# Attentions 3 and 4 of a four-layer perceiver: where a head's sums are folded and divided, and in which order TensorE issues a head's steps

## The reference, cut to what matters

```
q = (layernorm(x) @ Wq.T + bq) per head;  k = (ctx @ Wk.T + bk);  v = (ctx @ Wv.T + bv)
scores = q @ k.T / sqrt(16)                 # 256 x 4096 for each of 16 heads
attn   = softmax(scores, axis=-1)
x      = x + (attn @ v) @ Wo.T + bo
```

## Time and profile before

| what | value |
|---|---|
| median of 3 runs | 1447.46 us |
| profiled execution | 1446.92 us, its span 1445.7 us |
| TensorE / VectorE / ScalarE / GpSimd busy | 87% / 71% / 59% / 33% of the span |
| attention 3, from the first maximum to the last division | 927.28 to 1118.69 us |
| attention 4, the same | 1210.55 to 1401.97 us |
| VectorE busy from 953 to 1098 us | 139.1 of 145 us |
| granted TensorE clock from 953 to 1098 us | 1.00 |

### The profile page before, as it was taken

The page is one execution under the profiler, slowest core; times in us unless marked ns, Lnnn a source line. Parts: engine busy times, 40 slices in busy tenths (PEclk is TensorE's granted clock), DMA queues, the critical chain, the costliest instruction groups (busy, mean ns, idle before and its releaser), DMA issues. The chain is left out here.

```text
span 1445.7 us, 29634 instructions
## 1 busy us (share of the span) xinstructions
PE 1258.0 (87%) x10855; PEld 633.9 (44%) x10930; DVE 1020.2 (71%) x2341; ACT 851.7 (59%) x1339; POOL 482.2 (33%) x678
## 2 busy tenths in 40 slices
PE   6899786999998786799999888599998895999987
PEld 5566451333333355133333554244444582444445
DVE  4868578999998435788886153499994336999932
ACT  4632127999998330388888451178886212788852
POOL 1421314899889603244444240111110001111100
PEclk9999895999999989599999999789999997999999
DMA  8598781211122020111223336212144201122300
GB/s 319 157 318 291 217 296 42 56 38 38 44 58 97 3 72 22 46 41 54 56 51 124 124 71 218 65 47 65 56 126 142 73 0 43 56 64 67 114 2 8
DMA packets 115175, 136.62 MB, mean 95 GB/s; under 512 B 13579, under 2 KB 96179, under 8 KB 112956
## 3 DMA queue, kind: packets, MB, share of 16 engines
q1 hardware_dynamic: 107142, 126.55, 28.4%
q10 hardware_dynamic: 7888, 8.16, 1.7%
HBM read 99.73 MB, written 34.90 MB: 93 GB/s over the span
## 5 line engine op out<-in xcount | busy, mean ns | idle before, releaser
L1263 ACT ACTIVATE prob_a<-ps 128x1024 f32<-128x1024 f32 x480 | 468.6, 1020 | 97.4 <-PE ps L1086 57.4
L1068 PE MATMUL ps<-kop,qop 52*128 52x512 f16 x1024 | 302.2, 418 | 64.4 <-DMA qop<-qparts 21.3
L1287 DVE TENSOR_REDUCE best_a<-ps 128x1 f32<-128x512 f32 (+1 forms) x488 | 317.8, 709 | 25.0 <-PE ps L1068 22.9
L1086 PE MATMUL ps<-qop,kop 52*128 52x256 f16 x2048 | 217.8, 280 | 6.2 <-ACT prob_a L1263 2.7
L1115 PE MATMUL ps<-prob_a,vop_a 128*32 128x256 f32 x3072 | 212.8, 399 | 4.8 <-issue 4.7
L1283 DVE CUSTOM_DVE_ANT_0 dump_a<-ps,neg_q 128x512 bf16<-128x512 f32 (+1 forms) x244 | 165.8, 715 | 42.7 <-PE ps L1068 41.5
L1068 PEld LDWEIGHTS ps<-kop,qop 52*128 52x128 f16 x1024 | 73.1, 95 | 247.1 <-DVE best_a L1287 96.6
L1401 POOL TENSOR_TENSOR used_a<-prob_a,gT 128x1024 f32<-128x1024 f32 x64 | 154.1, 2409 | 24.0 <-DVE used_a L1300 19.4
L1379 POOL TENSOR_SCALAR mrest_a<-nmax_a 128x2 f32<-128x2 f32 x64 | 27.9, 435 | 332.9 <-DVE nmax_a L1292 332.9
L1086 PEld LDWEIGHTS ps<-qop,kop 52*128 52x128 f16 x2048 | 92.1, 96 | 105.6 <-issue 53.4
L1115 PEld LDWEIGHTS ps<-prob_a,vop_a 128*32 128x32 f32 x3072 | 86.0, 112 | 90.6 <-issue 58.1
(11 more groups left out here) (382 smaller groups left out, 1755.3 us busy)
## 6 DMA issues: line engine op xcount, KB each, us to landing
kop<-kparts SPq DMA_DIRECT2D x384, 64.0 KB, 2.3
vals<-vst SPq DMA_DIRECT2D x16, 1024.0 KB, 5.8
kparts<-kp SPq DMA_DIRECT2D x64, 256.0 KB, 4.2
vraw<-vals SPq DMA_DIRECT2D x64, 256.0 KB, 3.0
e_w<-in_e_w SPq DMA_DIRECT2D x4, 2048.0 KB, 11.5
z_w<-in_z_w SPq DMA_DIRECT2D x24, 256.0 KB, 7.0
gT<-in_ctxT SPq DMA_DIRECT2D x8, 512.0 KB, 12.5
raw<-in_mask SPq DMA_DIRECT2D x16, 256.0 KB, 3.9
```

Of the source, the lines that this page charges most:

```text
L1068: return pe.matmul(out, qop[rows, h, t * P:(t + 1) * P], kop[rows, h % UNROLL, first:first + CHUNK], start=True, stop=True)
L1086: ins = pe.matmul(st_bank(n)[:, j * NT:(j + 1) * NT], kop[rows, h % UNROLL, at:at + P], qop[rows, h, :], start=(j % 2 == 0), stop=(not add ...
L1263: act.activation(prob[:, n % NP, :], st_bank(n), ACT.Exp, scale=1.0 / SCORE_UNIT).then_inc(S("exp_done"), 1)
L1287: dve.tensor_reduce(out, bank, AX.X, ALU.max).then_inc(sem, 1)
```

## The change

Six edits, all for attentions 3 and 4 (`not by_query`):

- **F into bank 7.** For heads 0 to 14 (`aside`) the folded sums go into the first 64 columns of bank 7, over the sums that have been read, and not into the ring. F takes no place among the chunks any more.
- **ScalarE takes them out** (`read_fold`): one copy of 128 x 64 from PSUM to `folded_sums`, right behind `place_max`. V3 has to wait for it too, as it opens new sums in the same bank.
- **GpSimd divides** (`divide`): a power of -1 of the 128 x 2 denominators and a multiply of 128 x 32, behind the head's `split` and `fill`. The last head is divided by VectorE as before.
- **`AHEAD` is 26** and not 24: 13 pairs at the start, and the last chunk of head h+1 is now the 6th C of head h.
- **`TURN_AT` is 4** and not 5: `place_max` stands behind the fifth exponential of a head and not the sixth.
- **A new `PLAIN_ORDER`**: F and T stand together behind C10, V's are spread differently.

```diff
-PLAIN_ORDER = "CCKKCCV CKCKCCV KCKCF CCTCKKCV CCV".replace(" ", "")
+PLAIN_ORDER = "CCKKCV CKCCKCV CKCCFTKCCKCV CKCCV".replace(" ", "")
...
-    AHEAD = 32 if weighted else 24
+    AHEAD = 32 if weighted else 24 if by_query else 26
...
-    SUM_AT, TURN_AT = (1, 1) if weighted else (3, 4) if by_query else (3, 5)
+    SUM_AT, TURN_AT = (1, 1) if weighted else (3, 4) if by_query else (3, 4)
...
+    aside = lambda h: not by_query and h < H - 1
...
+    fold_out = c.ps[:, 7, 0:QT * 32]
...
                     if h > 0:
                         pe.wait_ge(S("sums_read"), h)
+                    if h > 0 and aside(h - 1):
+                        pe.wait_ge(S("fold_read"), h)
...
         def fold(h):
 
-            bank = ring_bank()
+            bank = fold_out if aside(h) else ring_bank()
             pe.wait_ge(S("sums_read"), h + 1)
...
-            ins.then_inc(S("s_psum"), 1)
+            ins.then_inc(S("folded" if aside(h) else "s_psum"), 1)
...
+        def read_fold(h):
+
+            act.wait_ge(S("folded"), h + 1)
+            if h > 1:
+                act.wait_ge(S("divided"), h - 1)
+            act.activation(folded_sums[:, h % 2, :, :], fold_out.rearrange("p (t e) -> p t e", t=QT), ACT.Copy)\
+               .then_inc(S("fold_read"), 1)
...
                 if g == TURN_AT and h + 1 < H:
                     place_max(h + 1)
+                if g == TURN_AT and h > 0 and aside(h - 1):
+                    read_fold(h - 1)
...
-                elif step == "F" and h > 0:
+                elif step == "F" and h > 0 and not aside(h - 1):
                     normalise(h - 1)
...
+        def divide(h):
+
+            pool.wait_ge(S("fold_read"), h + 1)
+            pool.tensor_tensor(rden[:, h % 2, :], folded_sums[:, h % 2, :, HD], minus_one[:, :], ALU.pow).then_inc(S("inverted"), 1)
+            pool.wait_ge(S("inverted"), h + 1)
+            pool.tensor_tensor(c.att[:, :, HD * h:HD * (h + 1)], folded_sums[:, h % 2, :, 0:HD],
+                               rden[:, h % 2, :].unsqueeze(2).to_broadcast((P, QT, HD)), ALU.mult).then_inc(S("divided"), 1)
...
             if not SHARED and 0 < h < H - 1:
                 fill(h + 1)
+            if h > 0 and aside(h - 1):
+                divide(h - 1)
```

More of the change, by code:

```diff
@@ L1002, in attend @@
     rden = sb("rden", [P, 2, QT], F32)
+    folded_sums = None if by_query else sb("folded_sums", [P, 2, QT, 32], F32)
+    minus_one = None if by_query else sb("minus_one", [P, QT], F32)
     dump = sb("dump", [P, 1, CHUNK] if weighted else [P, 2, 2 * CHUNK], BF16) if by_query else None
@@ L1194, in _ @@
         stage.reads = slots.n
+        stage.divided = 0 if by_query else H - 1
     @stage.scalar
@@ L1249, in _ @@
                     at += 1
-                if step == "F" and h > 0:
+                if step == "F" and h > 0 and not aside(h - 1):
                     slots.next()
@@ L1311, in normalise @@
                 dve.wait_ge(S("den_added"), h + 1)
+            if not by_query:
+                dve.wait_ge(S("divided"), H - 1)
             dve.reciprocal(rden[:, h % 2, :], den[:, h % 2, :] if weighted else folded[:, :, HD]).then_inc(S("den_inverted"), 1)
-            dve.wait_ge(S("den_inverted"), h + 1)
+            dve.wait_ge(S("den_inverted"), h + 1 if by_query else 1)
             dve.tensor_tensor(c.att[:, :, HD * h:HD * (h + 1)], folded[:, :, 0:HD],
@@ L1438, in _ @@
         pool.wait_ge(S("cleared"), 3)
+        if not by_query:
+            pool.memset(minus_one[:, :], -1.0).then_inc(S("cleared"), 1)
+            pool.wait_ge(S("cleared"), 4)
         fill(0)
@@ L1484, in _ @@
         pe.wait_ge(attended.S("s_read"), attended.reads)
+        if attended.divided:
+            pe.wait_ge(attended.S("divided"), attended.divided)
         turn_pe(c, pe, S, c.att, 0, "att_turned")
```

## The result

The changed kernel takes 1432.44 us (1427.49 to 1435.11, 5 runs) against 1447.46 for the kernel before, which had five runs here too, from 1441.00 to 1452.93 (the three named at the top are among them). The ratio is 0.9888, its 95% interval 0.9859 to 0.9916. The changed kernel is faster by 1.1%, and the forecast of 1434.5 stands 2 us off.

A forecast was written before the change was run, and what follows sets the result against it. VectorE was taken to set the pace. 13 periods x 0.54 = 7.0, less 0.5, made 6.5 us an attention, 13.0 for two: 1446.92 to 1433.9, and 1434.5 as the median lies 0.5 above; range 1429 to 1443.

The forecast's parts named there:

- The chain: Steps behind a head's maximum over chunks: T at 1.73 us, place_max 2.05, V3 3.17, C14 4.18, R14 4.60.
- The period: Time of one steady head: 9.60 + 0.31 + 0.21 + 0.16 = 10.28 us, 0.54 less than before.
- The wait of R14: VectorE's wait for the chunk behind V3: R14 due at 4.39 us, starting at 4.60, so 0.21 late.
- the maximum over chunks: VectorE's term per head for this step: 0.19 us plus 0.12 of waiting for the last chunk's semaphore, 0.31.
- The wait behind V1: VectorE's wait for chunk C4 behind V1: R4 due at 8.21 us, starting at 8.37, so 0.16 late.
- The division leaves VectorE: -0.30 a head: VectorE in a steady head: losing the division saves 0.30 us, with nothing new put there.
- read_fold: ScalarE's new copy of 64 columns behind place_max: 0.22 us, bounds 0 and 0.38, costing the chain 0.12.
- GpSimd: Division moved there: power 0.72 us, multiply between 0.20 and 1.27, at most 4.0 of 10.3 in all; nobody waits.
- the factor of two: Trainium skill's figure that GpSimd needs about twice VectorE's time; prediction said the power's 0.72 against 0.16 agrees.
- The start: Start of each attention, 13 pairs and not 12: 0 us change, bounds -0.5 and +1.0.
- The end: End of each attention, with 13 groups of keys left and not 12: +0.5 us, bounds 0 and 0.92.
- The clock rival: TensorE falls to 1.2 GHz in the steady stretch, about 1.45 us each drop; 9%, most of it slower than before.

The follow-up runs named there:

- one_last_wait: Changed kernel with two implied waits ahead of V3 left out on TensorE's queue and the read_fold wait put last: 1429.71 us, ratio 0.9882.
- ring_division: Changed kernel's new order, AHEAD 26 and TURN_AT 4, but fold back in the ring and division on VectorE: 1431.56 us, ratio 0.9893.
- vector_divides: Changed kernel, but VectorE divides from the copy in SBUF just ahead of R14 and GpSimd does not divide: 1435.16 us, ratio 0.9923.
- old_order_aside: Kernel before, with its old order, AHEAD 24 and TURN_AT 5, plus only the moved fold, read_fold and GpSimd division: 1460.27 us, ratio 1.0107.
- ahead24: Changed kernel with AHEAD 24 and not 26: 1503.76 us in one run, against 1451.93 for the kernel before.
- four_reads: Changed kernel in which ScalarE reads the folded sums four times instead of once: 1442.14 us in one run, against 1445.76 for the kernel before.
- both: Changed kernel with fewer waits ahead of V3 (one_last_wait) and the first pairs of chunks going round the banks in another order: 1427.42 us, ratio 0.9858.

## Why the prediction was right

The forecast was right in sign and size, and the chain that it was built on is what the traces show. One of its terms was no cause, and the nearness of the number is in part luck, as the last paragraph shows. One row of the kernel before is needed beside those above, VectorE's next one behind the maximum over chunks at 946.09:

```profile
946.18 3.29 DVE L1287 TENSOR_REDUCE best_a<-ps 128x1 f32<-128x512 f32 x5
```

Point by point:

- *The chain* was the step that carried it, and it held within 0.09 at each link. T came 0.08 earlier than forecast. V3 came 0.26 behind read_fold, where I took 0.09 from place_max: a second wait instruction stands on TensorE's queue behind the deciding one. one_last_wait shows 0.11 of the difference; the other 0.06 are open.
- *The period* was forecast 10.28 and is 10.34. The wait of R14 is 0.36 against its due time, not 0.21: 0.07 from the chain, the rest because the maximum over chunks costs VectorE 0.2 and not 0.31. In the earlier trace rows the 0.19 behind it hid a wait for C9; in the row above it is 0.09. The wait behind V1 was forecast 0.16 and is 0.14.
- *"The division leaves VectorE: -0.30 a head"* failed as a cause. The sum of terms was right, but it counted the 0.30 and the new wait of R14 as two facts. ring_division has the gain with the division on VectorE, vector_divides too, and old_order_aside loses with it gone. The gain is the order, that is the new string with `AHEAD` 26 and `TURN_AT` 4 (ahead24 shows that the string without `AHEAD` 26 loses; `TURN_AT` was not tried alone), and the three edits that move fold and division add 0.01. Before, R15 ended the chain at 4.48 and ten chunk maxima followed up to R8 and the next maximum over chunks, 6.34. Now R14 ends it at 4.67 and nine follow up to R6, 5.67. So the chain became 0.19 longer and what stands behind it 0.67 shorter, one chunk maximum and some waiting: 0.48 less. In ring_division R14 comes at 4.66, the division ahead of it, and the same 5.69 follow.
- *read_fold* took the forecast 0.22, and is on the path (four_reads: 0.35 a head for three more).
- *GpSimd*: the power takes 0.71 and the multiply 0.24, and nobody waits, as forecast. VectorE took 0.16 and 0.19 for the same two steps, so the first is 4.4 times as long on GpSimd and the second 1.3 times; neither is the factor of two that the prediction held the first against.
- *The start* was forecast 0 with +1.0 as a bound; it cost 0.5 and 1.7 in the profiled execution, 1.7 and 1.3 in the second, so three of four lie above the bound. The maximum came 0.8 later as said, but then V3 met the low clock for longer: the clock rose 25.1 and 27.8 us behind the first chunk's maximum, before it rose at 24.0 in both. The first period after that maximum was forecast near 11 and took 11.73 and 12.90.
- *The end* was forecast +0.5, and it became 0.3 and 1.4 shorter. TensorE's clock fell in other places: before, it stood at 1.2 GHz for 3.4 us twice in each end (in attention 3 from 1101.5 and from 1111.7); now it does so for 6.8 us at a stretch in attention 3 (from 1095.6) and for 3.4 us once in attention 4 (from 1375.5). In one_last_wait and both, whose clock does not fall there, the end takes 17.01. Start and end together: +0.5 forecast against +0.2 and +0.3. That they came out so near is luck, as both parts had it wrong.
- *The clock rival* did not occur; its price was right (1.45 against 1.6), and it occurs in three neighbours of this kernel (four_reads, old_order_aside, ahead24).

By the traces attention 3 gains 13 x 0.474 - 0.2 = 6.0 and attention 4 13 x 0.456 - 0.3 = 5.6, together 11.6, where 13.0 was forecast. The two profiled executions differ by as much (1446.92 and 1435.11, 11.8), but the changed kernel's is the slowest of its five. The medians differ by 15.0, with an interval of 4 us either way; whether the other 3 us are real is open. So the forecast lies between a saving of 11.6 and one of 15.0, and that it stands only 2 us from the median owes something to luck.

## What to carry to other kernels

When an engine looks full, first ask whether its waits sit at the end of a chain that starts from its own result. Then work taken off it turns into waiting, and what helps is to start the chain earlier or to put more of the engine's work beside it. Price each edit against the kernel without that edit, and not only the whole change against the old kernel: terms of a sum can be right while one of them is no cause. And look at single heads before you read a mean: four_reads has a mean period of 10.81, a value that stands for none of its heads: most take 10.69 and two take 12.24.

## What the runs showed of the hardware that was not expected

- A wait instruction that is already satisfied costs about 0.11 us on TensorE's queue if it stands behind the one that decides: V3 started 0.26 behind its releaser with one there (the changed kernel) and 0.15 without (one_last_wait).
- How near a kernel is to a fall of TensorE's clock did not show in its speed at full clock. Each fall made a head 1.3 to 1.6 us longer:

| kernel | usual head at full clock | idles of TensorE in it | heads with a fall, of 26 |
|---|---|---|---|
| changed | 10.34 | 0.24, 0.21 | 0 |
| before | 10.82 | 0.21, 0.15 | 0 |
| four_reads | 10.69 | 0.60, 0.20 | 2 |
| old_order_aside | 11.02 | 0.33, 0.56 | 5 |
| ahead24 | 11.62 | 1.38, 0.34 | 19 |

Each row is from one profiled execution, and the idles are those that the timeline shows. In four_reads and old_order_aside the heads with a fall have the same idles as those without, within a few hundredths, so what picks the head is not shown. A chain that is 0.2 to 0.35 us longer can so cost 1.6 in some heads.
